# Counting equal skills: from rounds of three batches to rounds of four, with GpSimd masking two of them

## The reference

```python
def step(carry, xs):
    att, cor = carry
    it, rt, vt = xs
    att = att.at[rows, it].add(vt.astype(jnp.int32))
    cor = cor.at[rows, it].add((rt * vt).astype(jnp.int32))
    return ((att, cor), (att[rows, it], cor[rows, it]))
...
attempts, correct, valid = _running_counts(q, r)
mastery = correct / jnp.maximum(attempts, 1.0)
skill_f = q.astype(jnp.float32)
s_enc = skill_f[..., None] * skill_w + skill_b
n_enc = attempts[..., None] * att_w + att_b
m_enc = mastery[..., None] * mast_w + mast_b
```

## Time and profile before

| | |
|---|---|
| median of 3 runs | 656.93 us (656.39 to 657.41) |
| the profiled execution | 657.44 us, its span 655.6 us |
| busy over the whole span | PE 609.0, DVE 530.2, ACT 426.3, POOL 358.0 us |
| granted clock of TensorE | 0.992 of full speed on average |
| counting stage | from 19.08 to 55.06 us |

### The profile page before, as it was taken

The page is one execution under the profiler, slowest core; times in us unless marked ns, Lnnn a source line. Parts: engine busy times, 40 slices in busy tenths (PEclk is TensorE's granted clock), DMA queues, the critical chain, the costliest instruction groups (busy, mean ns, idle before and its releaser), DMA issues.

```text
span 655.6 us, 18935 instructions
## 1 busy us (share of the span) xinstructions
PE 609.0 (93%) x5109; PEld 436.1 (67%) x5109; DVE 530.2 (81%) x1890; ACT 426.3 (65%) x1291; POOL 358.0 (55%) x441
## 2 busy tenths in 40 slices
PE   2484998799999999999999999999999999999997
PEld 0363776466677777777777777777777777777744
DVE  4998878765788888888888888888888888888675
ACT  6892776023567766667777667776666677776683
POOL 3001999414365555565666666655666566555654
PEclk9999998899999999999999999999999999999999
DMA  6300000100444444455455544444444444444364
GB/s 198 135 0 1 1 0 1 40 33 33 98 98 108 106 105 109 119 113 117 110 118 109 117 120 120 106 105 105 105 105 105 105 105 105 106 105 106 83 131 98
DMA packets 61623, 60.43 MB, mean 92 GB/s; under 512 B 22124, under 2 KB 57052, under 8 KB 61084
## 3 DMA queue, kind: packets, MB, share of 16 engines
q1 hardware_dynamic: 59164, 59.36, 37.8%
q10 hardware_dynamic: 2240, 0.73, 0.5%
q0 software_dynamic: 192, 0.01, 0.0%
HBM read 55.20 MB, written 4.89 MB: 92 GB/s over the span
## 4 chain that ended last, share of the span: by engine, by line
PE 87%; DVE 8%; issue 2%; ACT 1%; DMA 1%; SPq 0%; POOL 0%; DVEq 0%; ACTq 0%; POOLq 0%
PE bank L1614 16%; PE bank L1472 11%; PE bank L1595 9%; PE bank L1599 8%; PE bank L1537 5%; PE bank L1558 4%; PE bank L1494 3%; PE bank L1508 3%; PE bank L1513 3%; PE bank L1379 2%; PE bank L1483 2%; PE bank L1370 2%; PE bank L1462 2%; PE bank L1332 2%; PE bank L1361 2%
## 5 line engine op out<-in xcount | busy, mean ns | idle before, releaser
L687 ACT ACTIVATE skill_rows<-bank,b1T,w_scale 128x512 f32<-128x512 f32 x256 | 196.1, 778 | 8.4 <-PE bank L1599 6.6
L520 POOL TENSOR_TENSOR feat_parts<-skill_rows 128x512 f32<-128x512 f32 x62 | 79.0, 1275 | 93.8 <-DVE feat_parts L1047 88.9
L1614 PE MATMUL bank<-skill_rows,w_sb 128*64 128x256 f32 x928 | 122.7, 382 | 0.0
L1472 PE MATMUL bank<-feat_parts 128*128 128x128 f32 (+1 forms) x512 | 88.1, 306 | 2.5 <-DVE feat_parts L1030 1.2
L1614 PEld LDWEIGHTS bank<-skill_rows,w_sb 128*64 128x64 f32 x928 | 69.3, 137 | 27.2
L1472 PEld LDWEIGHTS bank<-feat_parts 128*128 128x128 f32 x512 | 78.1, 194 | 11.8 <-DVE feat_parts L1030 1.6
L1047 DVE TENSOR_TENSOR_SCAN feat_parts<-same,feat_parts 128x512 f32<-128x512 f32 x62 | 72.2, 1207 | 0.0
L1148 DVE SCALAR_TENSOR_TENSOR skill_rows<-bank,b2T,skill_rows 128x256 f32<-128x256 f32 x120 | 51.1, 477 | 16.3 <-PE bank L1614 13.4
L711 ACT ACTIVATE bank<-bank 128x64 f32<-128x64 f32 x128 | 26.7, 220 | 50.9 <-PE bank L1567 50.9
L1053 DVE TENSOR_TENSOR feat_parts<-bank,mask_sb 128x128 f32<-128x128 f32 x128 | 36.3, 285 | 28.6 <-PE bank L1472 27.3
L1148 DVE SCALAR_TENSOR_TENSOR skill_rows<-bank,b2T,feat_parts 128x256 f32<-128x256 f32 x112 | 47.6, 478 | 12.6 <-PE bank L1614 11.3
(11 more groups left out here) (284 smaller groups left out, 1506.8 us busy)
## 6 DMA issues: line engine op xcount, KB each, us to landing
skill_rows<-w_d SPq DMA_DIRECT2D x32, 512.0 KB, 6.3
same<-factor_d SPq DMA_DIRECT2D x31, 512.0 KB, 5.5
feat_parts<-w_d SPq DMA_DIRECT2D x30, 512.0 KB, 6.3
skill_rows<-skill_row_d SPq DMA_DIRECT2D x4, 1024.0 KB, 7.8
out<-o_sb SPq DMA_DIRECT2D x28, 128.0 KB, 5.2
feat_parts<-w_d SPq DMA_DIRECT2D x4, 256.0 KB, 4.9
w_sb<-in_L_ffn_W ACTq DMA_DIRECT2D x2, 256.0 KB
w_d<-wT SPq DMA_DIRECT2D x32, 16.0 KB, 1.4
```

What stands on the lines that cost most here:

```text
L520: pool.tensor_tensor(half[:, n, :], tm[:, 2 * n, :], tm[:, 2 * n + 1, :], ALU.add).then_inc(po_half, 1)
L687: act.activation(hid[:, e, :], banks[e % len(banks)][:, :], ACT.Gelu, bias=b1T[:, e:e + 1], scale=w1_scale[:, e:e + 1]).then_inc(ac_gelu, 1)
L1472: last = pe.matmul(n_bank[sc % 2][:, 0:SPAN[sc]], xs[:, k, sc * P:(sc + 1) * P], xs[:, k, sc * P:sc * P + SPAN[sc]], start=(k == 0), stop= ...
L1614: last = pe.matmul(z_bank[q % 2][n * D:(n + 1) * D, at:at + S // 2], w2_sb[:, e, :], hid[:, e, n * (S // 2):(n + 1) * (S // 2)], start=Tru ...
```

## The change

The counting goes in rounds of four (`FOURS` = 8, nothing left over). In round j:

- VectorE compares batches 4j, 4j + 1 and 4j + 2. It masks only the third (`whole_equal`) and, as before, ScalarE's (`own_only`).
- ScalarE makes batch 4j + 3.
- GpSimd masks 4j and 4j + 1 (`own_blocks`), each as soon as the four compares are made (`same_raw`).
- The third of VectorE's matrices has a buffer of its own, in the space of `feat_k`, which is not used before the features are turned.
- TensorE counts in the same order, and waits for GpSimd's masks on `same_in` and for VectorE's on a new semaphore, `same_own`.
- VectorE waits for the count of the batch four before, ahead of each compare.

```diff
-TRIPLES = B // 3
+FOURS = B // 4
...
         same = sb("same", [P, 2, C * (S + P)], BF16)
+        same_of = [same[:, 0, :], same[:, 1, :], feat_k[:, 0:C * (S + P)]]
...
-            pool.wait_ge(same_in, B)
+            def own_blocks(n, side):
+
+                pool.wait_ge(same_raw, C * (n + 1))
+                own = same_of[side].rearrange("p (c w) -> p c w", c=C)[:, :, 0:P]
+                pool.tensor_tensor(own, own, upto_b[:].unsqueeze(1).to_broadcast([P, C, P]), ALU.mult)\
+                    .then_inc(same_in, 1)
+
+            def four(j, side):
+                for n in range(2):
+                    own_blocks(2 * j + n, n)
+
+            four(0, 0)
+            four(1, 1)
+            with pool.Fori(1, FOURS // 2) as two:
+                four(2 * two, 0)
+                four(2 * two + 1, 1)
+            pool.wait_ge(same_own, 2 * FOURS)
...
             def equal(j, side):
-                wait(act, pe_counts, 3 * (j - 1))
+                wait(act, pe_counts, 4 * (j - 1))
...
-            def equal(b, side, n):
-                wait(dve, pe_counts, b - 2)
+            def compare(b, side, signal):
                 for sc in range(C):
-                    dve.tensor_scalar(same[:, side, sc * (S + P):(sc + 1) * S],
+                    dve.tensor_scalar(same_of[side][:, sc * (S + P):(sc + 1) * S],
                                       skill_rows[:, bass.ds(b * S + sc * P, WIDE[sc])],
-                                      skill_T[:, bass.ds(b * C + sc, 1)], None, ALU.is_equal).then_inc(same_raw, 1)
-                dve.wait_ge(same_raw, C * (n + 1))
-                own = same[:, side, :].rearrange("p (c w) -> p c w", c=C)[:, :, 0:P]
+                                      skill_T[:, bass.ds(b * C + sc, 1)], None, ALU.is_equal).then_inc(signal, 1)
+
+            def equal(j, n):
+                wait(dve, pe_counts, 4 * (j - 1) + n + 1 if not isinstance(j, int) or j else 0)
+                compare(4 * j + n, n, same_raw)
+
+            def whole_equal(j):
+                wait(dve, pe_counts, 4 * (j - 1) + 3 if not isinstance(j, int) or j else 0)
+                compare(4 * j + 2, 2, same_late)
+                dve.wait_ge(same_late, C * (j + 1))
+                own = same_of[2].rearrange("p (c w) -> p c w", c=C)[:, :, 0:P]
                 dve.tensor_tensor(own, own, upto_b[:].unsqueeze(1).to_broadcast([P, C, P]), ALU.mult)\
-                   .then_inc(same_in, 1)
+                   .then_inc(same_own, 1)
...
-            def three(j, side):
-                equal(3 * j, 0, 2 * j)
-                equal(3 * j + 1, 1, 2 * j + 1)
+            def four(j, side):
+                equal(j, 0)
+                equal(j, 1)
+                whole_equal(j)
                 own_only(j, side)
...
-            def three(j, side):
-                count(3 * j, of_dve(0))
-                count(3 * j + 1, of_dve(1))
-                count(3 * j + 2, of_act(side))
+            def four(j, side):
+                pe.wait_ge(same_in, 2 * j + 1)
+                count(4 * j, of_dve(0))
+                pe.wait_ge(same_in, 2 * j + 2)
+                count(4 * j + 1, of_dve(1))
+                pe.wait_ge(same_own, 2 * j + 1)
+                count(4 * j + 2, of_dve(2))
+                pe.wait_ge(same_own, 2 * j + 2)
+                count(4 * j + 3, of_act(side))
```

More of the change, by code:

```diff
@@ L226, in program @@
         tok_in = sem("tok_in")
-        same_raw, same_in, pe_counts = sem("same_raw"), sem("same_in"), sem("pe_counts")
+        same_raw, same_in, same_own, pe_counts = sem("same_raw"), sem("same_in"), sem("same_own"), sem("pe_counts")
+        same_late = sem("same_late")
         neg_in, gap_sq, gap_is = sem("neg_in"), sem("gap_sq"), sem("gap_is")
@@ L600, in equal @@
             def equal(j, side):
[L601 removed]
+                wait(act, pe_counts, 4 * (j - 1))
                 for sc in range(C):
                     act.activation(same_a[side][:, 0:C - sc, sc, :],
[L604 removed]
+                                   skill_rows[:, bass.ds((4 * j + 3) * S + sc * P, WIDE[sc])]
                                    .rearrange("p (j n) -> p j n", n=P),
[L606 removed]
+                                   ACT.Square, bias=neg_T[:, bass.ds((4 * j + 3) * C + sc, 1)]).then_inc(gap_sq, 1)
                 act.wait_ge(gap_sq, C * (j + 1))
@@ L616, in _ @@
                 act.wait_ge(ld_rows[q], 16)
-            with act.Fori(1, TRIPLES // 2) as two:
+            with act.Fori(1, FOURS // 2) as two:
                 equal(2 * two, 0)
@@ L867, in own_only @@
-            def own_only(n, side):
-                dve.wait_ge(gap_is, n + 1)
+                   .then_inc(same_own, 1)
+            def own_only(j, side):
+                dve.wait_ge(gap_is, j + 1)
                 own = same_a[side][:, 0]
                 dve.tensor_tensor(own, own, upto_b[:].unsqueeze(1).to_broadcast([P, C, P]), ALU.mult)\
-                   .then_inc(same_in, 1)
-            def three(j, side):
-                equal(3 * j, 0, 2 * j)
-                equal(3 * j + 1, 1, 2 * j + 1)
+                   .then_inc(same_own, 1)
@@ L876, in three @@
+            def four(j, side):
+                equal(j, 0)
+                equal(j, 1)
+                whole_equal(j)
                 own_only(j, side)
             dve.wait_ge(ld_rows[0], 16)
-            three(0, 0)
-            three(1, 1)
+            four(0, 0)
+            four(1, 1)
             for q in range(1, 4):
                 dve.wait_ge(ld_rows[q], 16)
-            with dve.Fori(1, TRIPLES // 2) as two:
-                three(2 * two, 0)
-                three(2 * two + 1, 1)
@@ L886, in _ @@
-            for n in range(B - 3 * TRIPLES):
-                equal(3 * TRIPLES + n, n, 2 * TRIPLES + n)
+            with dve.Fori(1, FOURS // 2) as two:
+                four(2 * two, 0)
+                four(2 * two + 1, 1)
             op(dve.tensor_scalar(valid[:], skill_T[:], 0.0, None, ALU.is_ge))
@@ L1337, in of_dve @@
             def of_dve(side):
-                return lambda sc, tc: same[:, side, sc * S + P * tc:sc * S + P * tc + P]
+                return lambda sc, tc: same_of[side][:, sc * S + P * tc:sc * S + P * tc + P]
             def of_act(side):
                 return lambda sc, tc: same_a[side][:, tc - sc, sc, :]
-            def three(j, side):
-                count(3 * j, of_dve(0))
-                count(3 * j + 1, of_dve(1))
-                count(3 * j + 2, of_act(side))
-            pe.wait_ge(tok_in, 1)
[L1349 to L1355, removed]
+            def four(j, side):
[7 more added lines that the diff above has]
+                count(4 * j + 3, of_act(side))
+            pe.wait_ge(tok_in, 1)
+            four(0, 0)
+            four(1, 1)
+            with pe.Fori(1, FOURS // 2) as two:
+                four(2 * two, 0)
+                four(2 * two + 1, 1)
             def features(g, side):
```

1 line of the change is left out of this document (removed).

## The result

The changed kernel takes 663.62 us (median of 4 runs, 663.46 to 665.34) against 656.66 for the kernel before on the same chips (4 runs, 655.71 to 657.41): a ratio of 1.0115, 95% interval 1.0095 to 1.0134. It is 7.0 us slower. The prediction said 668.0 us, with 658 to 674 for the range. The medians understate it a little: most executions of either kernel have a mean granted clock of 0.992 or 0.995, those at 0.992 take over 1 us longer, and at 0.995 the means are 663.57 us for three of the four changed ones and 655.53 for five of the kernel before (timed beside the first experiments), 8.0 us apart.

The account below looks back on a forecast made before the run. ScalarE and TensorE were taken to bound the counting stage; with GpSimd's masks holding VectorE, eight rounds of 5.7 us from 19.08, plus 1.15 and 0.15, put `attempts` at 66.2 against 55.06: +11.1, 668.0 us, range 658 to 674.

Parts of the forecast that it names:

- part collision: Rival: masks of 0.65 to 0.9 us, or only some VectorE work waiting; round 4.6 to 5.1, 659 to 663 us; 8 in 100.
- the exclusion of the forecast: Main case: GpSimd masks and VectorE operations shut each other out; round 5.2 to 6.1 us, 664 to 671 us; 64 in 100.
- Who bounds the stage: Counting stage before the change: ScalarE (3.4 us a round of three) and TensorE (3.3) bound it together, VectorE at 3.0.
- The gain of free masks, half a microsecond: If nothing collided, TensorE would pace the counting stage and `attempts` come at 54.6 against 55.06 us.
- TensorE's floor of 4.36 us a round: TensorE's least time for a round of four in the counting loop: 4 x 1.03 us and half a loop edge.
- The collision: Counting stage: each GpSimd mask holds up VectorE's SBUF work, as L1112 waited for a GpSimd product; L468 spoke against it.
- The length of a mask: A GpSimd mask in the counting stage: between 0.65 and 1.3 us, taken as 1.2.
- The hold: Time each GpSimd mask holds VectorE: 1.2 - 0.14 = 1.06 us, the 0.14 being what L1112 hid.
- VectorE's round without holds: VectorE's work in a round of four: 3 x 0.97 + 2 x 0.35 = 3.6 us.
- R: Length of a round of four: 3.6 + 2 x 1.06 = 5.7 us on VectorE; the change in time is 8R - 34.7.
- The tail: End of the counting stage, after VectorE's eight rounds: last hop and looped count 1.15 us, `attempts` 0.15.
- Starving: Rival: GpSimd gets in only when VectorE waits, so the round is 6.3 us, +16, 673 us; 13 in 100.

Follow-up runs that it names:

- masks back: The changed kernel with GpSimd's sixteen masks back on VectorE, rounds of four and three buffers kept: 657.58 us against 656.63 for the kernel before, ratio 1.0013.
- the powers: The kernel before plus sixteen GpSimd powers of 128x5 elements on an unused piece of `feat_k`: 656.9 us against 656.67, ratio 1.001.
- masks aside: The kernel before plus sixteen GpSimd masks on an unused piece of `feat_k`, on which no matrix or count depends: 670.49 us against 656.63, ratio 1.0207.

## Why the prediction was right

The range held 663.62 us, and the cause was the one forecast. The size was not: +7.0 us against +11.1. The time and the round stand on the border of two cases, just under the forecast's 664 us and 5.2 us, and just above the 663 and 5.1 of part collision; the rows say that it was the exclusion of the forecast, priced too high. Term by term:

*Who bounds the stage.* Right, and sharper after the runs: writing the loops out takes 0.9 us off the stage of before, and the next bound is ScalarE.

*The gain of free masks, half a microsecond.* Not borne out. The step that failed is TensorE's floor of 4.36 us a round, made of 4 x 1.03 and half an edge; it is 4.53, with gaps of 0.16 to 0.18 us ahead of three counts of a turn that the sum did not have. The 24 looped counts take 26.97 us in the run with masks back (29.16 to 56.13, with 0.30 of waiting for VectorE), where the sum had 25.7 and up to 0.6. An estimate for free masks, from the sum's own start of 28.5 and 26.7 to 27.0 for the loop, puts `attempts` at 55.3 to 55.6, after 55.06 and not before it. No run had free masks; with VectorE doing them the stage ends 1.1 us later than before.

*The collision.* Right, shown from several sides: by taking the masks off GpSimd (663.62 to 657.58, 6.0 us less), by adding them where nobody waits for them (656.63 to 670.49, 13.9 us more), and by a compare form that is not held. The choice to go by L1112 rather than by L468 was the right one. What the prediction says of L468, that it "hardly touches SBUF", agrees with the powers, 1.3 us long and without effect, but they are the same operation as L468, so the reason stays open.

*The length of a mask.* 1.19 us, said 1.2; but some 0.2 of it is the compare under way, by where the rows end.

*The hold.* 0.89 us (1204 against 313 ns for the 384-wide compare), said 1.06. The term allowed for 0.14 us hidden, as at L1112. Here a compare is under way when the mask starts and finishes undisturbed, and 0.3 is hidden.

*VectorE's round without holds.* 5.14 - 2 x 0.89 = 3.36 us, said 3.6. A set of compares followed by another set takes 0.86 us, not 0.97, since no mask waits for its last compare: (2.60 - 0.89) / 2 from 29.24 to 31.84 above. These two terms make R 5.14 instead of 5.7, worth 8 x 0.56 = 4.5 us; R lies just under the forecast's 5.2 to 6.1.

*The tail.* Said 1.30 us from the end of VectorE's masks to `attempts`, measured 2.14 (60.05, where `valid` begins, to 62.19). VectorE's two masks of a round come 0.34 us apart, so two looped counts of about 1 us stand one behind the other. The errors partly cancel, which is luck: -4.5 + 0.8, and the start 0.3 us earlier, leave 7.1 of the 11.1 us.

*Starving* did not happen: 14 of 16 masks have 1.19 us, the first 1.42, the second 1.29.

## What to carry to other kernels

In this kernel an idle GpSimd was no free engine beside a VectorE that works from SBUF, in its fast one-input form or with two inputs. Before work is moved there, look for a small VectorE operation whose maximum lies far over its minimum and ends with a GpSimd row; then count what is moved twice, once on GpSimd and once as a hold on VectorE. Here 0.35 us of VectorE work turned into 0.89 us of holding. And where three engines are level, taking work off one buys only the distance to the next: price the looped and register-driven instructions of that next one from a whole loop turn, not from single items.

## What the runs showed of the hardware

- A GpSimd memset holds VectorE's fast one-input forms before the stage too. In the run with masks aside, a cast on VectorE ends with the memset that fills 128x2560 (timeline):

```profile
6.55 2.24 POOL L430 MEMSET feat_k<- 128x2560 bf16 x1
6.93 1.94 DVE L823 CAST ident_h<-ident_f 128x128 f16<-128x128 f32 x1 [1.60 <-DMA dec<-in_decays]
```

  In the kernel before this cast takes 0.23 us. It begins 0.38 us into the memset and ends 0.08 after it.
- Four cases, then, for what holds what: a GpSimd product of 128x512 elements holds the fast one-input form and the two-input form of VectorE (1.2 and 1.4 us instead of 0.31 and 0.42); a memset only the one-input one (0.53 instead of 0.35 on average); a power of 5 elements neither; and the summing one-input form is not held by the product, the only one that it was tried with (0.74 both times). The Trainium skill (SBUF — State Buffer, § Who interferes with whom) sorts the first, second and fourth in the same way: one-input scalar operations can take the shared port pair unless they write out their accumulator, and a VectorE instruction with two SBUF inputs contends only with a GpSimd instruction that reads SBUF. The power does not fit it.
- Why a power of 1.3 us leaves VectorE free is open: it was tried with 5 elements only.
